# First feature tiles ahead of the short tile, and the first low rank projection inside the short tile's weights

## What is computed

```
def lora_add(base, inp, A, B):
    Ab = A[layer_idx][lora_indices]
    Bb = B[layer_idx][lora_indices]
    t = jnp.einsum('bri,bni->bnr', Ab, inp)
    return base + jnp.einsum('bor,bnr->bno', Bb, t) * SCALE
gate = lora_add(x @ W_gate.T, x, A_gate, B_gate)
up   = lora_add(x @ W_up.T,   x, A_up,   B_up)
act  = silu(gate) * up
c    = lora_add(act @ W_down.T, act, A_down, B_down)
nx   = c * rsqrt(mean(c * c) + eps) * ln_w
out  = x + (silu(nx @ gate_w.T) * (nx @ up_w.T)) @ down_w.T
```

## Time and profile before

| | |
|---|---|
| median of 3 runs | 418.76 us (418.23 to 419.34) |
| the profiled execution's own time | 419.01 us |
| its span, first to last instruction | 417.2 us |
| busy TensorE, VectorE, ScalarE | 98%, 77%, 56% of the span |

### The profile page before, as it was taken

The page is one execution under the profiler, slowest core; times in us unless marked ns, Lnnn a source line. Parts: engine busy times, 40 slices in busy tenths (PEclk is TensorE's granted clock), DMA queues, the critical chain, the costliest instruction groups (busy, mean ns, idle before and its releaser), DMA issues.

```text
span 417.2 us, 5385 instructions
## 1 busy us (share of the span) xinstructions
PE 408.6 (98%) x1824; PEld 337.5 (81%) x1824; DVE 322.0 (77%) x493; ACT 234.5 (56%) x369; POOL 12.5 (3%) x16
## 2 busy tenths in 40 slices
PE   5999999999999999999999999999999999999996
PEld 3888888888888888888888888888888888888885
DVE  5779867777785757643879988787887869899993
ACT  4577776565656348650655653645556567374740
POOL 9000000000000200000000000000000000000000
PEclk9999999999999999999999999999999999999999
DMA  7440044411011340020010113231213123305112
GB/s 272 151 132 0 9 133 131 127 44 57 24 52 53 90 118 22 20 82 0 0 52 0 51 57 128 69 102 50 103 50 101 44 97 116 124 2 190 50 50 101
DMA packets 13948, 31.86 MB, mean 76 GB/s; under 512 B 2274, under 2 KB 4706, under 8 KB 13922
## 3 DMA queue, kind: packets, MB, share of 16 engines
q1 hardware_dynamic: 13490, 31.01, 22.5%
q10 hardware_dynamic: 432, 0.52, 0.4%
HBM read 29.43 MB, written 2.10 MB: 76 GB/s over the span
## 4 chain that ended last, share of the span: by engine, by line
PE 94%; ACT 2%; issue 1%; DVE 1%; DMA 1%; DVEq 0%; ACTq 0%
PE bank L1268 43%; PE bank L1579 16%; PE bank L1444 14%; PE bank L1372 10%; PE bank L1402 3%; PE bank L1457 2%; PE bank L1278 2%; ACT stack L378 2%; PE bank L1409 1%; DMA xsum_c<-wsh_in 1%; DVE xs L1056 1%; DVE act L830 1%; PE bank L1464 0%; PE bank L1471 0%; DVE act L1224 0%
## 5 line engine op out<-in xcount | busy, mean ns | idle before, releaser
L1268 PE MATMUL bank<-xs,ws 128*128 128x512 f32 x840 | 194.8, 390 | 0.3
L1268 PEld LDWEIGHTS bank<-xs,ws 128*128 128x128 f32 x840 | 156.4, 188 | 33.2 <-DVE act L830 1.5
L1444 PE MATMUL bank<-xs,wdc 128*128 128x512 f32 x264 | 62.9, 389 | 0.0
L1444 PEld LDWEIGHTS bank<-xs,wdc 128*128 128x128 f32 x264 | 49.3, 188 | 10.1
L378 ACT ACTIVATE xs<-act 128x512 fp32r<-128x512 f32 x71 | 42.9, 624 | 21.2 <-DVE act L937 7.6
L787 DVE TENSOR_TENSOR xs<-act,xs 128x512 fp32r<-128x512 f32 x71 | 47.6, 686 | 4.7 <-ACT xs L378 4.1
L1372 PE MATMUL bank<-xs,ws 128*128 128x512 f32 x192 | 44.8, 390 | 0.0
L787 DVE TENSOR_TENSOR ws<-wraw,ws 128x256 fp32r<-128x256 f32 (+1 forms) x49 | 32.9, 682 | 14.2 <-ACT ws L378 14.0
L1372 PEld LDWEIGHTS bank<-xs,ws 128*128 128x128 f32 x192 | 35.7, 188 | 7.2
L378 ACT ACTIVATE bank<-bank 128x512 f32<-128x512 f32 x22 | 12.7, 580 | 45.7 <-PE bank L1268 45.7
L1579 PE MATMUL bank<-xs,vs 128*128 128x512 f32 x168 | 38.2, 389 | 0.0
(11 more groups left out here) (113 smaller groups left out, 396.3 us busy)
## 6 DMA issues: line engine op xcount, KB each, us to landing
wraw<-wgu_in SPq DMA_DIRECT2D x24, 512.0 KB, 3.3
wdr<-vs_in SPq DMA_DIRECT2D x7, 512.0 KB, 3.5
wdr<-wd_in SPq DMA_DIRECT2D x11, 256.0 KB, 2.7
wraw<-vj_in SPq DMA_DIRECT2D x3, 896.0 KB, 4.7
xa<-xT_in SPq DMA_DIRECT2D x3, 512.0 KB, 7.2
bgu_raw<-bgu_in SPq DMA_DIRECT2D x32, 32.0 KB, 1.9
xres<-xT_in SPq DMA_DIRECT2D x4, 256.0 KB, 3.9
act<-xT_in SPq DMA_DIRECT2D x4, 256.0 KB, 6.1
```

The source lines that it names most:

```text
L1268: ins = mm(z[:, :], ws[:, j % 2, w, s, k * P:(k + 1) * P], xs[:, c, r, k, :], start=(start and k == 0 and s == 0 and r == 0), stop=(k == 1 ...
L1444: ins = mm(z[:, :], wd[:, s, h * P:(h + 1) * P], x[r], start=(start and s == 0 and r == 0), stop=False, skip_group_check=True)
```

## The change

TensorE's order becomes: 10 matmuls on ones; `first_units`, tiles 0 and 5 of half 0 (48 matmuls), slice by slice, so that a slice of x and one of the weights are enough to begin; `short(0)`; `conv_0(2)`, tile 0 of half 1 (24 matmuls); the low rank matmuls of half 0 (`first_loras(0)`, 12 of 256 columns); `short(1)`; `conv_0(3)` (24); `first_loras(1)` (12); group 0 as before.

The 24 matmuls of the first low rank projection go. The short tile uses 96 of 128 weight columns; the 32 free ones now hold A of two samples, which are a pair q with 256 tokens. So each weight block exists for each pair, and `short(t)` is 48 matmuls of 256 columns for each half instead of 24 of 512. The result lies in partitions 96 to 127 of the short tile's banks; t_mask becomes two instructions of 32x512 for each half instead of four of 32x256.

The weights of tiles 0 and 5 come as four slices of 256 KB (`w0_in`) on ACT's queue instead of weights 0 and 1 on SP's; the short weights follow as one transfer. The indices move from SP's to ACT's queue, behind the first of these slices. On SP, the `agu` transfers now stand ahead of x of half 1. The lists of ACT and DVE are reordered, and POOL's memsets wait until the first weight slice is converted. Weight counts in the waits shift by 2. Cut to its core:

```diff
-WARM = 8
+WARM = 10
...
-UNITS = ((0, 0), (0, 1), (1, 0), (1, 1), (0, 0), (1, 0), (0, 1), (1, 1))
+UNITS = ((0, 0), (1, 0), (0, 1), (1, 1)) * 2
...
-        wsh = xs[:, XT1, :, :, :].rearrange("p s k n -> p (s k n)").rearrange(
-            "p (s k g m) -> p s k g m", s=2, g=2, k=KT)
-        wsh_pad = xs[:, XT1, :, :, :].rearrange("p s k n -> p (s k n)").rearrange("p (x m) -> p x m", m=P)[:, :, CR:P]
+        w0_flat = ws[:, 1, :, :, :].rearrange("p c s m -> p (c s m)")[:, 0:6 * 4 * P].rearrange("p (k s x) -> p k s x", k=3, s=2)
+        w0_raw = wraw[:, :, :, :].rearrange("p a b n -> p (a b n)").rearrange("p (k x) -> p k x", k=KT)
+        wsh = [part.rearrange("p (k g q m) -> p k g q m", k=KT, g=2, q=2)
+               for part in (xs[:, XT3, :, :, :].rearrange("p s k n -> p (s k n)"), wsh_lo[:, :])]
+        wsh_w = [part.rearrange("p k g q m -> p (k g) q m")[:, :, :, 0:CR] for part in wsh]
+        raw_kg = wsh_raw.rearrange("p k g m -> p (k g) m").unsqueeze(2).to_broadcast([P, 2 * KT, 2, CR])
+
+        def w0(s, k):
+            return w0_flat[:, k, s, :] if k < 3 else w0_3[:, s, :]
+
+        def w0_tile(s, k, g, i):
+            return w0(s, k)[:, (2 * g + i) * P:(2 * g + i + 1) * P]
+
+        def lora_a(s, b):
+            at = CR + RANK * (b % 2)
+            return wsh[s][:, :, :, b % 4 // 2, at:at + RANK].rearrange("p k g r -> p g k r")
...
-                if j >= 2:
-                    sp.wait_ge(s_walo, j - 1)
-                    sp.wait_ge(s_wblo, j - 1)
-                sp.dma_start(wraw[:, j % 2, :, :], wgu_in[j].rearrange("p (a m) -> p a m", a=4)
+                if j < 4:
+                    sp.wait_ge(s_w0lo, (2, 4)[j - 2])
+                else:
+                    sp.wait_ge(s_walo, j - 3)
+                    sp.wait_ge(s_wblo, j - 3)
+                sp.dma_start(wraw[:, j % 2, :, :], wgu_in[j - 2].rearrange("p (a m) -> p a m", a=4)
...
-            sp.dma_start(idx[:, :], idx_in[:, :]).then_inc(s_idx, 16)
-            for k in range(2):
-                sp.dma_start(xa1[:, 2 * k:2 * k + 2, :], xT_in[1, :, 2 * k:2 * k + 2, :]).then_inc(s_x1_ld[k], 16)
-            load_w(0)
-            load_w(1)
             sp.wait_ge(s_idx, 16)
             which = []
             for b in range(B):
                 which.append(sp.value_load(idx[0:1, b:b + 1], min_val=0, max_val=R - 1))
                 sp.dma_start(agu_raw[:, b], agu_in[ds(which[b], 1)].rearrange(
                     "o p (g k r) -> (o p) g k r", g=2, k=KT)).then_inc(s_agu_ld, 16)
+            for k in range(2):
+                sp.dma_start(xa1[:, 2 * k:2 * k + 2, :], xT_in[1, :, 2 * k:2 * k + 2, :]).then_inc(s_x1_ld[k], 16)
...
-            nc.scalar.dma_start(wsh_raw[:, 0], wsh_in[:, 0]).then_inc(s_wsh_ld[0], 16)
+            def load_w0(k):
+                nc.scalar.dma_start(w0_raw[:, k], w0_in[k]).then_inc(s_w0_ld[k], 16)
+
+            def hi_agu(b):
+                copy(lora_a(0, b), agu_raw[:, b]).then_inc(s_agu_hi, 1)
+
+            load_w0(0)
+            nc.scalar.dma_start(idx[:, :], idx_in[:, :]).then_inc(s_idx, 16)
             a.wait_ge(s_warm, 2)
             silu(stat[:, 1:2], stat[:, 0:1]).then_inc(s_table, 1)
-            nc.scalar.dma_start(wsh_raw[:, 1:KT], wsh_in[:, 1:KT]).then_inc(s_wsh_ld[1], 16)
+            for k in range(1, KT):
+                load_w0(k)
+            nc.scalar.dma_start(wsh_raw, wsh_in).then_inc(s_wsh_ld, 16)
             for k in range(KT):
+                if k >= 1:
+                    a.wait_ge(s_w0_ld[k], 16)
+                    copy(w0(0, k), w0_raw[:, k]).then_inc(s_w0hi, 1)
                 if k < 3:
                     a.wait_ge(s_x0_ld[k], 16)
                 copy(xs[:, (X11, X21)[k // 2], 0, k % 2, :], xa0[:, k, :]).then_inc(s_xhi[0], 1)
-                if k == 0:
-                    a.wait_ge(s_wsh_ld[1], 16)
-                    copy(wsh[:, 0, 1:KT, :, 0:CR], wsh_raw[:, 1:KT]).then_inc(s_wsh_hi, 1)
+            a.wait_ge(s_wsh_ld, 16)
+            for q in range(2):
+                copy(wsh_w[0][:, :, q, :], raw_kg[:, :, q, :]).then_inc(s_wsh_hi, 1)
+            a.wait_ge(s_agu_ld, 16 * B)
+            for b in range(4):
+                hi_agu(b)
             a.wait_ge(s_x1_ld[0], 16)
             hi_x(0, X12, xa1[:, 0:2, :])
             a.wait_ge(s_x1_ld[1], 16)
             hi_x(0, X22, xa1[:, 2:4, :])
-            hi_a(0)
-            hi_b(0)
-            a.wait_ge(s_agu_ld, 16 * B)
-            for b in range(B):
-                to = ag[:, b // 4, 0, :, :].rearrange("p k (g b r) -> p g k b r", g=2, b=4)
-                copy(to[:, :, :, b % 4, :], agu_raw[:, b]).then_inc(s_agu_hi, 1)
-            hi_a(1)
-            hi_b(1)
             stack_hi(0, 0)
+            a.wait_ge(s_xsum[0], 1)
+            hi_x(0, T_SLOT[0], xsum_c[:, 0])
+            a.wait_ge(s_short, 1)
+            for b in range(4, B):
+                hi_agu(b)
             t_hi(0)
-            stack_hi(0, 1)
-            t_hi(1)
-            a.wait_ge(s_short, 2)
-            for i in range(3):
-                a.wait_ge(s_xsum[0], i + 1)
-                hi_x(0, T_SLOT[i], xsum_c[:, i])
-                if i == 1:
-                    short_silu(0)
-                    short_silu(1)
+            a.wait_ge(s_xsum[0], 2)
+            hi_x(0, T_SLOT[1], xsum_c[:, 1])
             unit_silu(0)
             unit_silu(1)
+            short_silu(0)
+            stack_hi(0, 1)
+            hi_a(2)
             t_neg()
+            hi_b(2)
+            t_hi(1)
             stack_hi(1, 0)
+            a.wait_ge(s_short, 2)
+            a.wait_ge(s_xsum[0], 3)
+            hi_x(0, T_SLOT[2], xsum_c[:, 2])
             unit_silu(2)
+            unit_silu(3)
+            short_silu(1)
             stack_hi(1, 1)
-            unit_silu(3)
-            hi_a(2)
-            hi_b(2)
             a.wait_ge(s_xsum[0], 4)
             a.wait_ge(s_uu, 4)
             hi_x(0, XT4, xsum_c[:, 3])
...
-                v.wait_ge(s_ta, t + 1)
+                v.wait_ge(s_short, t + 1)
+                more = mask[96:P, 256:CH].unsqueeze(1).to_broadcast([32, 2, 256])
                 for g in range(2):
-                    for q in range(2):
-                        rows, cols = slice(64 * g + 32 * q, 64 * g + 32 * q + 32), slice(256 * q, 256 * q + 256)
-                        nc.vector.tensor_tensor(traw[32 * t:32 * t + 32, 2 * g + q, :], TA_BANK[t][rows, cols], mask[rows, cols], ALU.mult
-                                                ).then_inc(s_tm, 1)
+                    nc.vector.tensor_tensor(traw[32 * t:32 * t + 32, 2 * g:2 * g + 2, :],
+                                            SHORT_BANK[t][g][96:P, :].rearrange("p (q n) -> p q n", q=2), more, ALU.mult
+                                            ).then_inc(s_tm, 1)
...
-            v.wait_ge(s_wsh_ld[0], 16)
-            nc.vector.tensor_copy(wsh[:, 0, 0, :, 0:CR], wsh_raw[:, 0]).then_inc(s_wsh_hi0, 1)
-            v.wait_ge(s_wsh_hi0, 1)
-            sub(wsh[:, 1, 0, :, 0:CR], wsh_raw[:, 0], wsh[:, 0, 0, :, 0:CR]).then_inc(s_wsh_lo, 1)
+            def lo_agu(b):
+                v.wait_ge(s_agu_hi, b + 1)
+                sub(lora_a(1, b), agu_raw[:, b], lora_a(0, b)).then_inc(s_agu_lo, 1)
+
+            v.wait_ge(s_w0_ld[0], 16)
+            nc.vector.tensor_copy(w0(0, 0), w0_raw[:, 0]).then_inc(s_w0hi0, 1)
             for k in range(KT):
+                if k == 0:
+                    v.wait_ge(s_w0hi0, 1)
+                else:
+                    v.wait_ge(s_w0hi, k)
+                sub(w0(1, k), w0_raw[:, k], w0(0, k)).then_inc(s_w0lo, 1)
                 c = (X11, X21)[k // 2]
                 lo_x(0, k + 1, xs[:, c, 1, k % 2, :], xa0[:, k, :], xs[:, c, 0, k % 2, :])
-                if k == 0:
-                    v.wait_ge(s_wsh_hi, 1)
-                    sub(wsh[:, 1, 1:KT, :, 0:CR], wsh_raw[:, 1:KT], wsh[:, 0, 1:KT, :, 0:CR]).then_inc(s_wsh_lo, 1)
+            for q in range(2):
+                v.wait_ge(s_wsh_hi, q + 1)
+                sub(wsh_w[1][:, :, q, :], raw_kg[:, :, q, :], wsh_w[0][:, :, q, :]).then_inc(s_wsh_lo, 1)
+            for b in range(4):
+                lo_agu(b)
             lo_x(0, XC["12"], xs[:, X12, 1], xa1[:, 0:2, :], xs[:, X12, 0])
+            v.wait_ge(s_mask, 3)
+            nc.vector.tensor_copy(mask[96:P, 256:CH], mask[32:64, 256:CH]).then_inc(s_maskr, 1)
             lo_x(0, XC["22"], xs[:, X22, 1], xa1[:, 2:4, :], xs[:, X22, 0])
-            lo_a(0)
-            lo_b(0)
-            v.wait_ge(s_mask, 3)
-            nc.vector.tensor_copy(mask[64:P, :], mask[0:64, :]).then_inc(s_maskr, 1)
-            for b in range(B):
-                v.wait_ge(s_agu_hi, b + 1)
-                hl = [ag[:, b // 4, s, :, :].rearrange("p k (g b r) -> p g k b r", g=2, b=4)[:, :, :, b % 4, :] for s in range(2)]
-                sub(hl[1], agu_raw[:, b], hl[0]).then_inc(s_agu_lo, 1)
-            lo_a(1)
-            lo_b(1)
             v.wait_ge(s_wsh_lo, 2)
             x_sum(0, 0)
+            stack_lo(0, 0)
```

(147 more changed lines are left out.)

83 lines of the change are left out of this document (45 added, 38 removed).

## The result

The changed kernel takes 425.38 us (median of 4 runs, 423.80 to 426.53) against 418.82 (418.23 to 419.34) for the kernel before: ratio 1.0154, 95% interval 1.0115 to 1.0194, so 6.6 us slower. The profiled execution took 426.08 us, with a span of 424.2 against 417.2. It starts p4(0) at 70.88 instead of 63.77, 7.1 us later, so the whole difference arises ahead of that point.

A forecast was written before the change was run, and what follows sets the result against it. VectorE's list behind the stack, reached through SP and ScalarE, was to decide. 1.0 for the chain plus 2.5 and 0.7 for the clock gave 4.2 us: 419.0 becomes 423.2, less 0.25, 422.9 us; range 418.0 to 426.5.

The forecast's parts named there:

- the sum: Total loss: p4(0) 1.0 us later, plus 2.5 and 0.7 us for clock falls, 4.2 us slower.
- The path: Chain from SP over ScalarE's stack copy and VectorE's list to `ca(0)` and p4(0): p4(0) starts 1.0 us later.
- both gaps: TensorE idle before the first low rank matmuls, 3.7 us, and before p6(0), 6.3 us; the clock falls in both.
- Rival 3: At the start, the index lands at 7.1 as before: 424.8 us, or up to 426.5; chance 0.06.
- the clock: TensorE's clock falls in its two gaps; slow matmuls afterwards cost 2.5 us and 0.7 us.
- step 4: Forced waits within VectorE's list: 0.95 at `t_lo(1)`, 1.96 at `lo_t(0,2)`, 0.1 at `t_lo(0)`; 3.0 us, `x_sum(0,3)` ending at 54.1.
- step 1: SP's queue: index lands at 5.2, `agu` issues from 6.14, `load_stack(0)` starts at 15.5, stack ready at 21.3.
- the second gap: TensorE idle from g of group 0 to `ca(0)`'s end, 6.3 us; clock climb behind it costs 2.5 us (0 to 3.4).
- the first gap: TensorE idle from `conv_0(2)`'s end to `t_lo(0)`'s end, 3.7 us; clock cost behind it 0.7 us (0 to 1.5).
- Rival 1: TensorE still decides up to `ca(0)`, gaining 9.4 us: 409.4 us in full, 416 in part; chance 0.14.
- step 3: VectorE's list from `stack_lo(0,0)` to `x_sum(0,3)`: 26.74 us of work.

The follow-up runs named there:

- the first experiment: The changed kernel with the two transfers of x of half 1 issued ahead of the wait for the index: 421.46 us, ratio 1.0063.
- the filling experiment: The changed kernel with 24 useless matmuls on ones between g of group 0 and p6(0): 423.35 us, ratio 1.0117.
- the split kernel: The kernel before with each of the short tile's 48 matmuls split into two of 256 columns: 419.56 us, ratio 1.0019.

## Why the prediction was right

422.9 was forecast, 425.4 measured, in the range of 418.0 to 426.5 and on the side that was given 0.72. It lies 0.4 above the 420.5 to 425 that were given 0.66, and the sum was 4.2 us for 6.6 measured. The path and both gaps were the forecast ones; one term of the path was mis-sized by a mechanism that the prediction had left out, and others by less, all to the same side, so nothing cancelled. Rival 3 also covered this time, but it isn't what happened: the index came early. Its landing was a guess between 4.5 and 7.1, and that the `agu` issues began within 0.15 us of it was in part luck. The steps, with the time of each:

| step | predicted | measured |
|---|---|---|
| first real matmul | 6.3 | 6.01 |
| first `agu` issue | 6.14 | 5.99 |
| start of the stack's issues | 15.5 | 15.10 |
| stack ready for ScalarE | 21.3 | 23.06 |
| `x_sum(0,3)` ends | 54.1 | 57.30 |
| `ca(0)` begins | 55.2 | 58.30 |
| p4(0) starts (64.7 predicted, and 3.2 for the clock) | 67.9 | 70.88 |

**What held.** The new bound is VectorE's list behind the stack, `ca(0)` is where it reaches TensorE, both gaps are there (4.8 and 6.05 us for 3.7 and 6.3), and the clock falls in both. The forced waits of step 4 came out at 0.96 and 2.04 for 0.95 and 1.96.

**What failed: step 1, the term from the stack's issues to its use.** I took 5.83 us from the earlier trace rows and let "the two transfers moved in front" cost only their issue time, 1.2. They are also 1 MB in the same queue. The stack's eight transfers took 1.9 us each from issue to landing before, in the median, and 4.0 behind them, and the term became 7.96. The share of the transfer engines from 15 to 20 us is 0.90 in the changed kernel:

```profile
15.00:20.00 5.00, 5.00 (x33) 4.50 (x32) 1.15 (x5) 1.97 (x5) 0.00 (x0) 1.00 0.90 267
```

It was 0.31 in the kernel before. The term is 2.1 us longer than forecast; the issues started 0.4 earlier, so 1.8 of it is left of the 2.9 us by which the profile passes the forecast's 4.2, and the first experiment gives the 1.9 us of landing back. VectorE's list is another 0.8 (1.5 longer than summed, of which the 0.7 had been put down to the clock) and the way from `ca(0)` to p4(0) 0.5 (12.58 for 9.56 and 2.5). The trace agrees with a delay (the stack's first transfer took 4.4 us), though not with a strict order of landing: that transfer, issued at 15.1, was there at 19.5, and the second of x, issued at 14.5, only at 20.6. I had not used the rule. That the order within the queue is the cause, and not simply the load on the transfer engines, is argued: no run put the 1 MB on another queue.

**The clock.** Behind the second gap I took 2.5 us out of 0 to 3.4. The 18 matmuls show 7.03 less 4.08, 2.95 us, and the filling experiment 2.6 in the profile and 2.0 in the median. Behind the first gap I took 0.7 out of 0 to 1.5, at `t_mask(1)`. It showed 1.0, but in another place, which I had not named: the low rank matmuls themselves ran slowly, and `unit_mul(0)`, `unit_mul(1)` and `short_act(0)` waited 0.27, 0.16 and 0.59 us for the silus behind them, in the middle of the list that decides.

**TensorE's terms.** `short(0)` took 5.75 us for the 5.73 summed, and the split kernel's 0.3 to 1.3 us holds the 0.58. One sentence of the prediction is wrong as it stands, "the half matmul is 0.0121 us dearer than half a whole one": that is the price of a pair, 0.006 for each half; the sum uses it rightly. `conv_0(2)` ended at 29.18 for 28.3 summed, and 0.5 of that is the first 12 matmuls, 3.25 us for 2.72; it is ahead of a gap and costs nothing there. That the start costs nothing while the chain decides isn't shown by an experiment of its own. Rival 1's 409.4, TensorE alone, was near the right price for what could be had: 411.96 was reached with 1.5 us of gaps left, so some 410.5 without them, by an estimate. Its condition, a chain that ends before `ca(0)` is wanted, was not met by this change.

**What stays open.** Of the 1.5 us that step 3 and 4 were short by, 1.0 is shown above; the other 0.5 was not taken apart.

## What to carry to other kernels

When the engine that bounds a stage gets less to do, walk the lists of the other engines instruction by instruction, from the last load that starts them: here an estimated 9.4 us saved on TensorE turned into 6.6 us lost, and came back as 7.0 gained when only the order of the others' work and of the transfers was changed. A transfer whose data is wanted late still costs its bytes to everything issued behind it in its queue, not only its issue time. And a gap on TensorE like those of 4.8 and 6.05 us here is paid twice, once as a wait and once as slow matmuls after it.
